# A gated slot attention layer and its feed-forward part on one core: feed-forward steps begun inside the drain, and three orders of work changed

## The reference, cut to what matters

```
x: (B=4, T=512, 256)                      # H=16 heads of 128
q, k, v, w = silu(conv4(x @ W...))        # w l2-normalised; v and w share one filter
g = log_sigmoid(x @ Wf1 @ Wf2); beta = sigmoid(x @ Wb)
for t:                                    # per sequence and head
    Sk = Sk * exp(g_t) + k_t (x) beta_t w_t
    Sv = Sv * exp(g_t) + beta_t w_t (x) v_t
    o_t = softmax(q_t Sk / sqrt(128)) Sv
o = rmsnorm(o) * norm_w * sigmoid(x @ Wg1 @ Wg2 + bg2)
x = layernorm(x + o @ Wo)
f = (silu(x @ w_gate * s_gate) * (x @ w_up * s_up)) @ w_down * s_down   # int8 weights, 1024 wide
x = layernorm(x + f)
```

## Time and profile before

| | |
|---|---|
| median of 3 runs | 2012.46 us (2009.84 to 2013.88) |
| the profiled execution: its own time | 2009.03 us |
| its span | 2007.3 us, 41500 instructions |
| TensorE busy | 1927.6 us (96%) |
| VectorE, ScalarE, GpSimd busy | 1775.8 (88%), 1396.5 (70%), 1334.0 (66%) |
| mean granted TensorE clock | 0.984 |
| the chain that ended last | PE 82%, POOL 8%, DVE 5%, issue 3% |

### The profile page before, as it was taken

The page is one execution under the profiler, slowest core; times in us unless marked ns, Lnnn a source line. Parts: engine busy times, 40 slices in busy tenths (PEclk is TensorE's granted clock), DMA queues, the critical chain, the costliest instruction groups (busy, mean ns, idle before and its releaser), DMA issues.

```text
span 2007.3 us, 41500 instructions
## 1 busy us (share of the span) xinstructions
PE 1927.6 (96%) x12192; PEld 1627.1 (81%) x12192; DVE 1775.8 (88%) x4096; ACT 1396.5 (70%) x3986; POOL 1334.0 (66%) x2289
## 2 busy tenths in 40 slices
PE   7899999999999999999999999999999999999697
PEld 5688888888888888888888888888888888887586
DVE  5599999999999999999999999999999999998487
ACT  4477777777777777777777777777777777776442
POOL 5367676767677676777677776777676766766343
PEclk8899999999999999999999999999999999999798
DMA  3011110111111111111111111111110111102300
GB/s 78 1 55 26 25 35 14 36 24 33 26 24 26 26 34 23 27 24 32 26 27 23 27 34 24 26 24 33 26 34 15 29 32 23 22 15 51 63 11 32
DMA packets 53645, 58.51 MB, mean 29 GB/s; under 512 B 14896, under 2 KB 44720, under 8 KB 53424
## 3 DMA queue, kind: packets, MB, share of 16 engines
q0 software_dynamic: 9216, 33.56, 11.4%
q1 hardware_dynamic: 44208, 22.29, 4.0%
HBM read 20.19 MB, written 37.75 MB: 29 GB/s over the span
## 4 chain that ended last, share of the span: by engine, by line
PE 82%; POOL 8%; DVE 5%; issue 3%; ACT 1%; DMA 1%; POOLq 0%; DVEq 0%; ACTq 0%
PE proj_ps L718 15%; PE mix_ps L802 11%; PE V_ps L773 10%; PE work_ps L927 8%; PE work_ps L933 7%; PE tr_ps L742 6%; PE V_ps L751 5%; PE work_ps L1569 5%; PE proj_ps L397 4%; PE work_ps L822 3%; PE mix_ps L809 2%; POOL w_lo L370 2%; PE tr_ps L782 2%; PE work_ps L824 2%; POOL qk L618 1%
## 5 line engine op out<-in xcount | busy, mean ns | idle before, releaser
L587 DVE SCALAR_TENSOR_TENSOR conv<-proj_ps,coefs,conv 128x511 f32<-128x511 f32 (+2 forms) x768 | 561.9, 732 | 9.5 <-ACT conv L347 2.6
L298 POOL TENSOR_TENSOR W<-W,tot 128x256 f32<-128x256 f32 x384 | 256.0, 667 | 244.0 <-PE mix_ps L802 243.9
L1053 POOL TENSOR_TENSOR A_lev<-A,masks 128x256 f32<-128x256 f32 x448 | 319.5, 718 | 0.1
L802 PE MATMUL mix_ps<-W,U 128*128 128x128 f32 x1792 | 295.3, 287 | 13.7 <-POOL W L298 8.2
L802 PEld LDWEIGHTS mix_ps<-W,U 128*128 128x128 f32 x1792 | 256.5, 192 | 40.2 <-issue 24.5
L773 PE MATMUL V_ps<-A_lev,UT 128*128 128x128 f32 x1792 | 285.9, 282 | 1.6 <-DVE V_ps L683 1.6
L711 DVE COPY_PREDICATED A<-masks,mix_ps 128x256 f32<-128x256 uint32 x448 | 268.7, 600 | 12.3 <-PE mix_ps L802 12.2
L580 DVE TENSOR_TENSOR wT<-wT,tot 128x128 f32<-128x128 f32 x768 | 233.3, 344 | 40.3 <-DVE U L563 1.8
L773 PEld LDWEIGHTS V_ps<-A_lev,UT 128*128 128x128 f32 x1792 | 237.4, 192 | 23.4 <-DVE V_ps L683 23.2
L356 ACT ACTIVATE th<-conv 128x512 f32<-128x512 f32 x256 | 162.3, 634 | 104.2 <-DVE conv L587 103.0
L718 PE MATMUL proj_ps<-hT_hi,w_hi 128*128 128x512 f32 x512 | 222.9, 435 | 4.5 <-DVE conv L587 2.7
(11 more groups left out here) (200 smaller groups left out, 4774.0 us busy)
## 6 DMA issues: line engine op xcount, KB each, us to landing
head_sum<-y_sb POOLq DMA_DIRECT2D x64, 512.0 KB, 6.5
w_raw<-in_L_attn_Ww SPq DMA_DIRECT2D x16, 128.0 KB, 2.2
w_raw<-in_L_attn_Wq SPq DMA_DIRECT2D x16, 128.0 KB, 2.2
w_raw<-in_L_attn_Wk SPq DMA_DIRECT2D x16, 128.0 KB, 2.3
w_raw<-in_L_attn_Wv SPq DMA_DIRECT2D x16, 128.0 KB, 2.2
wo_raw<-in_L_attn_Wo SPq DMA_DIRECT2D x16, 128.0 KB, 2.0
head_sum<-in_L_attn_hidden_states SPq DMA_DIRECT2D x1, 2048.0 KB, 10.3
acc<-head_sum SPq DMA_DIRECT2D x4, 512.0 KB, 3.9
```

The source lines that it names most:

```text
L298: nc.gpsimd.tensor_tensor(w, w, block_tot(u3.par, lev, 0), ALU.mult).then_inc(W_step, 1)
L587: nc.vector.scalar_tensor_tensor(y_, proj_ps[:, CONV_BANK[i], 0:T - back], filt(u, i, KW - 1 - back), y_, ALU.mult, ALU.add).then_inc(conv ...
L802: last = nc.tensor.matmul(mix_ps[:, half, p * P:(p + 1) * P], Ulev(u3, lev)[:, p * P:(p + 1) * P], after_odd(W[:, p * T // 2:(p + 1) * T / ...
L1053: nc.gpsimd.tensor_tensor(dst, diag_after_odd(lev), mask_cols(lev), ALU.mult)\
```

## The change

Nothing of what is computed changes. TensorE's gate and up products of steps 0 and 1 are issued at the end of tail 1 and at r == 5 of tail 2, and the loop begins with step 2. The gate's banks, those of the down sums and those of the turned sequences 1 and 2 are exchanged, so that the early products have free banks. The scaling and the addition of unit 63 move into step 1, the normalising of sequence 1 and the statistics of sequence 2 into the loop; sequences are turned at steps 3, 6 and 11, not 1, 3 and 7. In tail 1 `largest` goes ahead of `attention_norm(0)`, the squares ahead of the casts, the scales and the clearing of the first banks behind `lows(0)`. `final_norm` of sequence 2 goes behind the loop. In the filling `beta_rows(1)` goes behind the last tap of slot 0, `low_x(2)` ahead of `descend` of level 1, and `high_x(3)` and `low_x(3)` one level ahead.

```diff
--- before.py
+++ after.py
@@ -319,7 +319,7 @@
         def ffn_gate_ps(f):
-            return proj_ps[:, f % 2, :]
+            return proj_ps[:, (f + 1) % 2, :]
@@ -431,13 +431,15 @@
         def down_bank(b, half):
-            return (work_ps[:, half, :] if b % 2 == 0 else (tr_ps, V_ps)[half][:, :])
+            return (work_ps[:, half, :] if b % 2 else (tr_ps, V_ps)[half][:, :])
...
-        def turn_bank(k):
-            return (tr_ps, V_ps)[k][:, :]
+        def turn_bank(b, k):
+            return work_ps[:, k, :] if b in (1, 2) else (tr_ps, V_ps)[k][:, :]
+
+        TURN_AT = {3: 1, 6: 2, 11: 3}
@@ -464,15 +466,13 @@
         def clear_down(dve, b):
-            if b == 0:
-                dve.wait_ge(ys_done, 4 * B * H)
-            elif b == 1:
-                dve.wait_ge(ffn["yT_lo"], B * KT)
+            if b < 3:
+                dve.wait_ge(ffn["yT_lo"], (1, 3, 4)[b] * KT)
@@ -519,15 +519,19 @@
         def turn_y(pe, b):
             pe.wait_ge(ffn["norm"], b * C + C)
             wait(pe, ffn["yT_lo"], b * KT)
+            if b == 1:
+                pe.wait_ge(ys_done, 4 * B * H)
+            if b == 3:
+                pe.wait_ge(ffn["res"], C)
@@ -1041,8 +1045,10 @@
-                    if s.u5 and i == 0:
+                    if s.u5 and s.tail < 3 and i == 0:
                         add_heads_output(pool, s.u5)
+                    if s.tail == 2 and i == 0:
+                        attention_rstd(pool, 1)
@@ -1102,15 +1108,17 @@
-                if s.tail in (0, 1, 3):
-                    attention_rstd(pool, (0, 1, None, 2)[s.tail])
+                if s.tail == 0:
+                    attention_rstd(pool, 0)
             for i in range(STEPS):
+                if i in (3, 7):
+                    attention_rstd(pool, (2, 3)[i // 7])
                 pool.wait_ge(ffn["fused_hi"], i + 1)
...
-                if i == 3:
-                    attention_rstd(pool, 3)
+                if i == 1:
+                    add_heads_output(pool, Unit(B * H - 1))
@@ -1141,13 +1149,6 @@
-                if s.tail == 1:
-
-                    act.wait_ge(ffn["q_in"], 48)
-                    for i, dst in enumerate((wg_r, wu_r, wd_r)):
...
-                    highs(act, 0)
@@ -1183,6 +1184,13 @@
+                    if s.tail == 1 and r == 0:
+
+                        act.wait_ge(ffn["q_in"], 48)
+                        for i, dst in enumerate((wg_r, wu_r, wd_r)):
...
+                        highs(act, 0)
@@ -1195,14 +1203,14 @@
+                    if s.n == 1 and r == 1:
+                        high_x(act, 3)
                     if u2 and r == 2:
                         values(act, u2)
                     if u1 and r == 2:
                         gates(act, u1)
...
-                    if s.n == 1 and r == 2:
-                        high_x(act, 3)
@@ -1243,7 +1251,7 @@
-                    if u4 and r in (6, 7):
+                    if u4 and s.tail != 2 and r in (6, 7):
@@ -1280,8 +1288,11 @@
-                if i in (1, 3, 7):
-                    highs(act, (1, 2, 3)[i // 3])
+                if i == 1:
+                    for t in range(C):
+                        scale_output(act, Unit(B * H - 1), t)
+                if i in TURN_AT:
+                    highs(act, TURN_AT[i])
@@ -1296,10 +1307,10 @@
+                if u3 and not (u1 and u1.h and u1.par == 0):
+                    largest(dve, u3)
                 if s.tail == 1:
                     attention_norm(dve, 0)
-                if u3 and not (u1 and u1.h and u1.par == 0):
-                    largest(dve, u3)
@@ -1314,6 +1325,8 @@
                     mix(dve, 0)
+                if s.n == 1:
+                    low_x(dve, 2)
                 if u2:
                     descend(dve, u2, 1)
...
-                    if s.n == 1 and r == 1:
-                        low_x(dve, 2)
...
                     if s.n == 1 and r == 2:
                         first_lows(dve, 2)
                         beta_rows(dve, 2)
+                        low_x(dve, 3)
...
-                    if s.n == 1 and r == 3:
-                        low_x(dve, 3)
...
-                    if s.n < 2 and r == 7:
-                        beta_rows(dve, (1, 3)[s.n])
+                    if s.n == 1 and r == 7:
+                        beta_rows(dve, 3)
@@ -1368,6 +1378,11 @@
                     if s.tail == 1 and r == 5:
                         lows(dve, 0)
+                        dve.wait_ge(ffn["scale_in"], 48)
+                        nc.vector.tensor_tensor(sgu[:, :], sg_sb[:, :], su_sb[:, :], ALU.mult).then_inc(ffn["scales"], 1)
...
+                        clear_down(dve, 0)
@@ -1383,6 +1398,8 @@
+                    if s.n == 0 and r == 8:
+                        beta_rows(dve, 1)
@@ -1396,15 +1413,7 @@
-                if s.tail == 2:
-                    attention_norm(dve, 1)
-                    attention_stats(dve, 2)
-
-            dve.wait_ge(ffn["scale_in"], 48)
...
-            clear_down(dve, 0)
@@ -1416,14 +1425,12 @@
-                if i == 0:
-                    attention_norm(dve, 2)
-                if i == 2:
-                    attention_stats(dve, 3)
-                if i == 4:
-                    attention_norm(dve, 3)
-                if i in (1, 3, 7):
-                    lows(dve, (1, 2, 3)[i // 3])
+                if i in (1, 4, 8):
+                    attention_norm(dve, (1, 2, 3)[i // 4])
+                if i in (3, 7):
+                    attention_stats(dve, (2, 3)[i // 7])
+                if i in TURN_AT:
+                    lows(dve, TURN_AT[i])
...
-                if b and f == 5:
+                if 0 < b < B - 1 and f == 5:
                     final_norm(dve, b - 1)
+            final_norm(dve, B - 2)
             for c in range(C):
                 residual(dve, B - 1, c)
@@ -1443,13 +1451,42 @@
+            def gate_and_up(i):
+
+                b, f = i // FT, i % FT
+                if i == 0:
+                    pe.wait_ge(ffn["cast"], 3)
+                if i == 1:
+                    pe.wait_ge(tg_done, B * H)
+                wait(pe, ffn["fused"], i - 1)
+                if f == 0:
+                    pe.wait_ge(ffn["yT_lo"], KT * (b + 1))
+                for w, dst in ((wg_r, ffn_gate_ps(i)), (wu_r, ffn_up_ps(i))):
...
-                if s.edge:
+                if s.edge and s.tail < 3:
@@ -1557,6 +1594,8 @@
+                    if s.tail == 2 and r == 5:
+                        gate_and_up(1)
                     if u4 and r in (5, 6):
@@ -1596,35 +1635,15 @@
+                if s.tail == 1:
+                    gate_and_up(0)
...
-            pe.wait_ge(ffn["cast"], 3)
...
             for i in range(STEPS):
...
+                if i > 1:
+                    gate_and_up(i)
+                if i in TURN_AT:
+                    turn_y(pe, TURN_AT[i])
                 if i >= 2:
                     down(i - 2)
```

52 lines of the change are left out of this document (22 added, 30 removed).

## The result

The changed kernel takes 1988.73 us, the median of four runs (1987.3 to 1990.4), beside 2012.57 us (2009.84 to 2013.88) for the kernel before: a ratio of 0.9885, with a 95% interval from 0.9872 to 0.9897. The forecast was 1992, some 20 us less than before; the medians differ by 23.8. The profiled execution took 1987.3 us with a span of 1985.6, against 2009.03 and 2007.3, so 21.7 us of span are to be found. Busy times hardly moved: TensorE 1921.0 us (97%) for 1927.6, VectorE 1774.2 for 1775.8. What went is waiting and half clock.

The account below looks back on a forecast made before the run. TensorE was taken to bound the steady slots, so only filling, drain and feed-forward loop could give time: 8.0 + 12.4 = 20.4, taken as 20, so 1992 us against the median of 2012.46; range 1984 to 2001.

Parts of the forecast that it names:

- Step 1: Filling: moving beta_rows(1) out of the tap chain TensorE waits for gains 0.75 us, bounds 0.55 and 0.8.
- step 2: Filling: low_x(2) issued earlier removes TensorE's whole 3.0 us wait, plus 1.5 us for a spared fall to half clock.
- Step 3: Filling: high_x(3) and low_x(3) moved ahead let TensorE start its products at 68.8, not 71.65: 2.8 us.
- rival D: Steady slots: the filling shifts the engines' phase and the slot gets longer; at 0.4 us a slot 2016 us; chance 0.04.
- step 4: Drain: largest ahead of attention_norm(0) on VectorE gains 2.1 us on the path exponentials, W, mix.
- step 5: Drain: squares of unit 62 ahead of the casts and highs(0) on ScalarE end TensorE's wait for W: 4.0 us.
- step 6: Drain, tail slot 1: scales and two memsets now stand ahead of the gating of tg, giving back 1.4 us.
- step 7: Drain: gate and up of the loop's first two steps issued early, 3.75 us of TensorE, covering 1.1 us of waiting.
- step 8: Loop: norm, statistics and turning move in; VectorE's load and the wait for residual 3 lose 2.9 us.
- Rival B: Loop: VectorE bounds it, GpSimd and VectorE blocking each other in nine places, 8 to 11 us; 2001 us; chance 0.12.
- step 9: End: final_norm(2) leaving step 29 of the loop makes fused(30) ready earlier and the end 2.4 us earlier.
- rival A: The forecast itself: gaps go, the loop loses about 3 us to VectorE; 13 to 27 us gained; chance 0.75.

Follow-up runs that it names:

- run 3: Changed kernel with only low_x(2) put back behind the slot's first taps; ratio to the kernel before 0.9908.
- run 2: Changed kernel with the filling's moves undone (beta_rows(1), low_x(2), high_x(3) and low_x(3) in their old places); ratio to the kernel before 0.9941.
- Run 5: Changed kernel with the three casts and highs(0) ahead of the squares of unit 62 on ScalarE again; ratio to the kernel before 0.9927.
- run 6: Changed kernel with gate and up of loop steps 0 and 1 issued behind the last slot again; ratio to the kernel before 0.9908.
- run 10: Changed kernel with sequence 3 turned at loop step 13 in place of 11; ratio to the kernel before 0.9887.
- run 4: Changed kernel with attention_norm(0) ahead of largest again on VectorE in tail slot 1; ratio to the kernel before 0.9915.
- run 8: Changed kernel with the scales and clear_down(0) moved behind the gating of tg in tail slot 1; ratio to the kernel before 0.9896.
- run 9: Changed kernel with final_norm(2) put back into step 29 of the loop on VectorE; ratio to the kernel before 0.9900.
- run 1: The changed kernel itself, unaltered, measured again beside the variants; ratio to the kernel before 0.9899.
- run 7: Changed kernel with the output scaling of unit 63 back in tail slot 2, ahead of tanh(0), on ScalarE; ratio to the kernel before 0.9920.

## Why the prediction was right, and where its terms were off

**Filling, steps 1 to 3: 8.0 forecast, 7.9 in the two profiles (7.6 from "start").** Step 1 gave 0.55 us, its lower bound: the first projection comes 11.05 us after "start" (36.48) for 11.60. The wait of step 2 went from 3.01 to 0.31 us, VectorE being ready at 47.8 instead of the 48.7 worked out, and TensorE there at 47.6. Step 3's wait is gone. The clock term of 1.5 us is not shown: the fall behind that wait went, but others came (run 3), and over the filling the half clock held no shorter than before. Against 6.5 us of waits the eleven profiles with the moves lie on average 6.1 us under the one of before and 8.9 under run 2. That 8.0 and 7.9 agree so well is luck of two profiles, of which the one after had 3.4 us less of half clock there. That the gain would cross 60 slots unharmed held in every profile, and rival D, a longer slot, had nothing behind it.

**Drain, steps 4 to 7: 12.9 forecast, 16.1 in the profiles, 15.4 with the mean of six.** The orders were priced well: 2.14 us for step 4 (2.1), a wait of 4.03 for step 5 (4.0), 1.0 to 1.3 for step 6 (1.4, given away). From the scores to the gate's last projection (L397: 1884.61 before, 1869.68 after) 7.0 us were won for 4.7, from there to gate(2) 9.1 for 8.2. The term that was mis-sized is the clock, which I bounded by -3.3 and +3 and took as 0. With the gaps closed it was at the full level from about 1863 and steps 0 and 1 ran at full rate (1.00 from 1866 to 1874, above), where before it was the half one until 1882 or 1883. From the first product with tg to that projection, the same products, it takes 4.4 us for 6.0: 1.6 of the 2.3 us. Run 5 shows the tie: with the 4 us gap back the half clock lasts past 1874. The other part is step 7, where I had counted 1.1 us of waiting covered by the early steps; run 6 measures about 2, since each wait also costs the overlap of the products on its two sides.

**Loop, step 8: 2.9 us lost in the forecast, 4.8 in the profiles, 5.2 with the mean.** The failing piece is the sentence "turn_y(3) waits for residual 3, which I find 1.8 us after TensorE arrives". It was 3.94. I had priced the four residuals at 3.4 us, 0.42 for each of their eight instructions. Ahead of the change they took just that (1926.51 to 1931.15); now two of the four additions take 1.1 to 1.2 us, beside GpSimd's fused_lo, as VectorE's and GpSimd's timelines of the changed kernel show:

```profile
1904.34 0.42 DVE L483 SCALAR_TENSOR_TENSOR acc<-tr_ps,sd_sb 128x256 f32<-128x256 f32 x1
1904.38 1.29 POOL L1118 TENSOR_TENSOR fused_lo<-fused,fused_hi 128x512 fp32r<-128x512 f32 x1 [2.28 <-ACT fused_hi L1281]
1904.79 1.16 DVE L485 TENSOR_TENSOR acc<-acc,y 128x256 f32<-128x256 f32 x1
...
1908.49 1.12 DVE L485 TENSOR_TENSOR acc<-acc,y 128x256 f32<-128x256 f32 x1
```

That is 1.4 of the 2.1 us; where the other 0.7 came from is not shown. The product from PSUM (L483) keeps its 0.42 us also while fused_lo runs. The rule that I held against the change thus bit in a place I had not priced. The Trainium skill, SBUF — State Buffer, "Who interferes with whom", also says that a VectorE instruction with two inputs in SBUF contends with GpSimd's reads, and that one with at most one, outside the modes that use two ports, does not. That is what L485 and L483 show here. fused_lo itself was hardly held up: 1.26 to 1.38 us in the whole loop, 1.27 to 1.38 before. Rival B needed that and nine places; what it has right is that VectorE bounds steps 9 to 13 (run 10).

I had not counted the second cost of a wait here either. After 3.94 us of idling the clock falls at 1911 and the products of gate(12) start 0.43 us apart, not 0.23. From gate(11) to gate(13) it takes 12.2 us there, of which 5.6 are two steps, 0.9 the turning and 3.9 the wait: 1.8 us are left for the half clock, and about one more in runs 2, 4, 8 and 9. All of the 4.8 us is lost by gate(16): steps 8 to 15 took 29.4 us (1895.04 to 1924.46), where I had said about 25.

**End, step 9: 2.4 forecast, 2.5 measured, 1.5 of it by the order.** Run 9 splits it. I had reasoned from the wait alone and got the size by luck: the half clock behind it in the one profile made up the difference.

The two mis-sized terms had opposite signs, +3.2 in the drain and -1.9 in the loop, so the sum of 20.4 came within 1.3 us of the 21.7. That they cancelled so far is luck; the mechanism, gaps closed and about 3 us lost to VectorE, is rival A's, with the loss too small.

## What to carry to other kernels

A gap of TensorE costs more than its length: count the wait, a few tenths of overlap lost on its two sides, and a half clock behind it whose length differs from run to run; the same gap can cost 2.5 us in one execution and 1.5 in another. When work moves into a loop, price each VectorE instruction that reads two operands from SBUF at its price beside GpSimd, and look at which instruction of the chain it stands ahead of; TensorE's own order (a turning two steps later) is the cheaper cure. With runs of one kernel 3 to 7 us apart, single changes of 1 to 4 us are read from stretches between common events, against several profiles of unchanged stretches, and only then from the times.

## What the runs showed of the hardware

The fall of the clock is not a fixed property of the program. Behind a wait of 2.53 us the last 16 products ran at the half clock in the kernel before (0.41 us each but the last two) and behind 2.52 us at the full clock in run 9 (0.28 us). At the wait for sequence 3, always 3.9 to 4.0 us, the fall came while TensorE still stood idle in runs 1, 2, 3, 4, 8 and 9 (up to 1.6 us before its next product, in run 8), and 1.2 us after that product's start in the changed kernel. The half clock then held for about 6.8 us in runs 2, 4, 8 and 9 and for 3.4 in the six others; gate(2) to gate(31) is 92.6 to 92.9 in those four and 91.5 to 91.8 in the rest, but for run 7, where the clock fell twice. In the drain the clock fell in every profile behind a wait for aN of 2.4 us or more and stayed down through a stretch in which TensorE was busy 4.00 us of 4 (1858 to 1862 in the changed kernel, at 0.50).

The kernel as a whole shows it too: five runs of variant 2 lie at 2000.4, 1998.5, 1996.5, 1995.0 and 1993.7 us of span, with mean granted clocks of 0.982, 0.983, 0.985, 0.986 and 0.987 in that order. What made these differ from one another, with the same program on the same chip, stays open.
